# A graph network kernel: node attention with the sources on the partitions, in strips of five destination tiles

## What is computed

```python
def gat_conv(x, src, dst, W, a_src, a_dst, b):
    h = x @ W
    s = h @ a_src
    d = h @ a_dst
    alpha = jax.nn.leaky_relu(s[src] + d[dst], NEG_SLOPE)
    n = h.shape[0]
    m = jax.ops.segment_max(alpha, dst, num_segments=n)
    ex = jnp.exp(alpha - m[dst])
    denom = jax.ops.segment_sum(ex, dst, num_segments=n)
    w = ex / (denom[dst] + 1e-16)
    out = jax.ops.segment_sum(h[src] * w[:, None], dst, num_segments=n)
    return out + b
```

## Time and profile before

| | us |
|---|---|
| median of 3 runs | 5927.24 |
| lowest and highest | 5904.29, 5947.91 |
| span of the profiled execution | 5765.0 |
| `count_edges`, first DVE step to the end of its stores | 792.6 to 1648 |
| node attention, layers 1, 2, 3, first DVE step to the last | 399.9, 401.1, 401.8 |

### The profile page before, as it was taken

One profiled execution on the slowest core, in us unless ns is written; L12 is line 12 of the kernel. 1 busy time (PEld: TensorE's weight loads), 2 busy tenths in 40 slices (PEclk: granted clock), 3 DMA queues, 4 the chain that ended last, 5 costly groups with the idle time before them and its releaser, 6 DMA issues. The chain is left out here.

```text
span 5765.0 us, 88635 instructions
## 1 busy us (share of the span) xinstructions
PE 4607.2 (80%) x24482; PEld 3873.4 (67%) x24483; DVE 2716.3 (47%) x5068; ACT 2120.2 (37%) x3279; POOL 836.5 (15%) x769
## 2 busy tenths in 40 slices
PE   3888868888856499669589989899769959969666
PEld 2677645555545399438578778788659959969555
DVE  5555567777653400321379689689631140020233
ACT  2333215544433200424256566566524420020332
POOL 2778710000005200002100000000022200000000
PEclk8788889999968799789799999999779979989878
DMA  3433311211113342113211111111122134224000
GB/s 97 113 111 106 101 37 71 79 71 75 66 62 100 106 161 109 30 34 116 65 51 56 46 44 55 42 49 55 39 71 97 36 93 162 109 92 159 36 17 24
DMA packets 150165, 438.52 MB, mean 76 GB/s; under 512 B 25592, under 2 KB 89805, under 8 KB 133676
## 3 DMA queue, kind: packets, MB, share of 16 engines
q1 hardware_dynamic: 115212, 341.23, 16.7%
q0 software_dynamic: 34848, 96.08, 5.9%
HBM read 340.98 MB, written 96.25 MB: 76 GB/s over the span
## 5 line engine op out<-in xcount | busy, mean ns | idle before, releaser
L2404 PE MATMUL p_acc<-p_H,p_eT 125*125 125x256 f32 x3750 | 823.5, 378 | 0.0
L2404 PEld LDWEIGHTS p_acc<-p_H,p_eT 125*125 125x125 f32 x3750 | 695.2, 187 | 106.0
L1033 POOL DMA_INDIRECT p_message<-edge_table,p_index x425 | 503.8, 1185 | 131.2 <-issue 120.9
L1951 DVE TENSOR_REDUCE p_mean<-F 128x1 f32<-128x3125 f32 x10 | 34.0, 3403 | 931.7 <-PEq L83 931.7
L1246 PE MATMUL p_acc<-p_message,p_spread 125*125 125x260 f32 x1666 | 425.6, 422 | 28.7 <-issue 28.7
L1298 POOL IOTA p_order_i<- 125x200 int32 x3 | 1.1, 381 | 2882.6 <-SPq L81 2882.6
L1705 ACT ACTIVATE p_hid<-p_up,p_b1s 128x125 f32<-128x125 f32 x764 | 273.0, 366 | 395.6 <-PE p_up L1681 352.5
L1246 PEld LDWEIGHTS p_acc<-p_message,p_spread 125*125 125x125 f32 x1666 | 348.4, 211 | 98.1 <-issue 30.6
L1681 PEld LDWEIGHTS p_up<-p_xT,p_w1s 128*128 128x128 f32 x3056 | 377.8, 199 | 51.3 <-issue 33.1
L1681 PE MATMUL p_up<-p_xT,p_w1s 128*128 128x125 f32 x3056 | 385.5, 283 | 32.9 <-issue 11.8
L835 PE MATMUL p_acc<-p_cell,p_heavy 125*125 (+1 forms) x1440 | 405.4, 392 | 0.0
(11 more groups left out here) (441 smaller groups left out, 8080.0 us busy)
## 6 DMA issues: line engine op xcount, KB each, us to landing
sums_first<-edge_sums SPq DMA_DIRECT2D x48, 1250.0 KB
p_second<-edge_sums SPq DMA_DIRECT2D x48, 1250.0 KB, 6.7
p_count<-edge_counts SPq DMA_DIRECT2D x75, 762.9 KB
edge_sums<-p_sums SPq DMA_DIRECT2D x32, 1250.0 KB, 4.4
edge_counts<-p_total SPq DMA_DIRECT2D x32, 610.4 KB
p_w1s<-in_L_ffn_W SPq DMA_DIRECT2D x16, 1024.0 KB
p_got<-made SPq DMA_DIRECT2D x25, 560.0 KB
p_dst_all<-dst_row SPq DMA_DIRECT2D x25, 531.2 KB
```

The lines of the kernel that those rows point to most:

```text
L1033: pool.indirect_dma_start(message[:, m, k, :], None, table, bass.IndirectOffsetOnAxis(ap=index[:, m, k:k + 1], axis=0)).then_inc(landed[m] ...
L1951: then(dve.tensor_reduce(mean[:, h:h + 1], F[:, h], AX_X, ALU.add))
L2404: last = pe.matmul(acc[:, s, 0:C], eT[:, r % 4, a % 4], H[:, a, 0:C], start=(a == 0), stop=(a == T - 1))
```

## The change

**In `attend_nodes` the matrix is made with the sources on the partitions.** A block of it is 125 sources x 125 destinations, and it goes straight into PE as the stationary side: there are no transposes and no copies behind them. The destinations are taken in strips of 5 tiles (625 columns), the sources in pieces of 5 tiles, so that a layer has 5 strips x 5 pieces = 25 pieces, each of 5 x 5 blocks. The five tiles of a strip accumulate in five PSUM banks. The peak over the sources is still taken with the destinations on the partitions (`mask`, one instruction of 3125 columns per tile, on a bf16 penalty that now comes from DRAM). Two row vectors per strip, peak - d and peak - 0.2 d (`limits`), are turned from the partitions to the columns of all partitions by PE with a diagonal matrix and ones (`spread_limits`), and ACT copies them to `steep` and `flat`. For each block row of 625 columns ACT makes steep - s, not below 0 (`steeps`), DVE takes the minimum with flat - 0.2 s (`join`), ACT makes exp(-x) for a piece (`exponents`), and DVE limits it to 1 and multiplies by the counts (`weigh`). The denominator is a column of ones ahead of H (POOL writes it), so a product has 257 columns. The feature tensor XT serves as two of the four buffers of pieces. H is projected from XT directly, without the copies of L2236.

**In `count_edges`** ACT makes a third copy of each block, `number`, from the same bank as `present`. SP stores `number` as a second table with the sources on the rows (`cells`, 128 x 25 runs of 100 uint16 each per group), and `keeps(j)` waits until the store of group j-1 has landed, since there is one buffer. The turned counts become a penalty, BIG where there is no edge, stored as bf16, and the turning is a bf16 product with the identity.

The diff, with the removed body of `attend_nodes`, the lists of semaphores and small tensors, the unchanged start of the stage and the callers left out:

```diff
--- before.py
+++ after.py
...
-def count_edges(nc, g, counts, weights):
...
@@ -751,9 +751,11 @@
...
-        turned = ph.sb("turned", [P, T, GD])
+        present = ph.sb("present", [P, T, GD], BF16)
+        number = ph.sb("number", [ROWS, T, GD], U16)
+        big = ph.sb("big", [P, 1])
         sums = ph.sb("sums", [ROWS, 2, T, GD])
-        total = ph.sb("total", [GD, N], U16)
+        penalty = ph.sb("penalty", [GD, N], BF16)
...
@@ -780,6 +783,8 @@
...
             dve.memset(sums[:], 0.0).then_inc(cleared, 1)
+            dve.memset(number[:], 0).then_inc(cleared, 1)
+            dve.memset(big[:], BIG).then_inc(cleared, 1)
...
@@ -875,7 +880,7 @@
...
-                        last = pe.transpose(flip[:, f % 4, (h - a) * P:(h - a + 1) * P], turned[:, h], g.ident[0:P, 0:P])
+                        last = pe.matmul(flip[:, f % 4, (h - a) * P:(h - a + 1) * P], present[:, h], ident16[:], start=True, stop=True)
...
@@ -897,14 +902,15 @@
...
-            act.wait_ge(cleared, 1)
+            act.wait_ge(cleared, 3)
             def keeps(j, i, m):
...
+                act.wait_ge(cells_stored, j * 16 + 16)
...
-                    for out, h in ((turned, 0), (sums[0:P, m], 1)):
+                    for out, h in ((present, 0), (number[0:P], 0), (sums[0:P, m], 1)):
                         last = act.activation(out[:, :, s * BLK:s * BLK + BLK].rearrange("p h d -> p d h"),
                                               acc[:, turn_of(nc, b), h, 0:BLK * T].rearrange("p a (d h) -> p (a d) h", h=T), ACT.Copy)
...
@@ -913,7 +919,8 @@
...
-                    act.activation(total[:, a * P:e * P], flip[:, f % 4, 0:(e - a) * P], ACT.Copy).then_inc(flip_kept, 1)
+                    act.activation(penalty[:, a * P:e * P], flip[:, f % 4, 0:(e - a) * P], ACT.Relu, scale=-BIG, bias=big[0:GD, 0:1]).then_inc(flip_kept, 1)
...
@@ -928,6 +935,7 @@
...
+            sp.sem_inc(cells_stored, 16)
...
@@ -935,10 +943,12 @@
...
                     sp.dma_start(weights[bass.ds(j * ROWS, ROWS), :], sums[:, m].rearrange("p h d -> p (h d)")).then_inc(sums_stored[m], 16)
+                    sp.dma_start(cells[:, :, bass.ds(j * GD, GD)], number[:]).then_inc(cells_stored, 16)
...
-                    sp.dma_start(counts[bass.ds(j * GD, GD), :], total[:]).then_inc(stored, 16)
+                    sp.dma_start(absent[bass.ds(j * GD, GD), :], penalty[:]).then_inc(stored, 16)
...
+            sp.wait_ge(cells_stored, 16 * GROUPS + 16)
             sp.wait_ge(stored, 16 * GROUPS + 16)
...
@@ -2134,277 +2144,298 @@
...
-def attend_nodes(nc, g, counts, XT, loads, turn, last, out):
...
+STRIP = 5
+STRIPS = T // STRIP
+SW = STRIP * P
+PIECE = 5
+PIECES_OF = T // PIECE
+MASKS = 8
+SLOTS_OF = 4
+def attend_nodes(nc, g, absent, cells, XT, loads, turn, last, out):
+    PIECES_ALL = STRIPS * PIECES_OF
+    HALVES = ((0, 3 * P), (3 * P, 2 * P))
...
+        H = ph.sb("H", [P, T, C + 3])
...
+        none = ph.sb("none", [128, 2, N], BF16)
...
+        cell = ph.sb("cell", [ROWS, 2, PIECE, SW], U16)
+        room = ph.sb("room", [P, 2, PIECE, SW])
+        gap = (room[:, 0], room[:, 1]) + tuple(XT[0:P, h].rearrange("p (k d) -> p k d", k=PIECE) for h in range(KH))
...
+        flat = ph.sb("flat", [P, 2, SW])
+        diag = ph.sb("diag", [P, 2, STRIP, P])
...
+            def load_none(t):
+                if t >= 2:
+                    sp.wait_ge(masked, t - 1)
+                sp.dma_start(none[:, t % 2], absent[t * P:t * P + 128, :]).then_inc(none_loaded[t % 2], 16)
+            def load_cell(n):
+                k, q = divmod(n, PIECES_OF)
+                if n >= 2:
+                    sp.wait_ge(weighed, (n - 1) * PIECE)
+                sp.dma_start(cell[:, n % 2], cells[:, q * PIECE:(q + 1) * PIECE, k * SW:(k + 1) * SW]).then_inc(cell_loaded[n % 2], 16)
+            load_none(0)
+            load_none(1)
+            load_cell(0)
+            load_cell(1)
+            for t in range(2, MASKS + 2):
+                load_none(t)
+            for n in range(PIECES_ALL - 2):
+                if MASKS + 2 + n < T:
+                    load_none(MASKS + 2 + n)
+                load_cell(n + 2)
...
+            def mask(t):
+                dve.wait_ge(none_loaded[t % 2], (t // 2 + 1) * 16)
+                if t:
+                    dve.wait_ge(masked, t)
+                dve.tensor_tensor_reduce(out=masked_by[:], in0=S[:], in1=none[0:P, t % 2], scale=1.0, scalar=-2.0 * BIG,
+                                         op0=ALU.subtract, op1=ALU.max, accum_out=peak[:, t:t + 1]).then_inc(masked, 1)
+            def limits(k):
+                t = k * STRIP
+                d = H[:, t:t + STRIP, C + 2]
+                dve.wait_ge(masked, t + STRIP)
+                dve.wait_ge(h_kept, t + STRIP)
+                then_small(dve.tensor_tensor(top[:], peak[:, t:t + STRIP], d, ALU.add))
+                then_small(dve.scalar_tensor_tensor(out=top[:], in0=top[:], scalar=0.2, in1=top[:], op0=ALU.mult, op1=ALU.max))
+                then_small(dve.tensor_scalar(any_edge[:], peak[:, t:t + STRIP], -0.5 * BIG, None, ALU.is_ge))
+                then_small(dve.tensor_tensor(top[:], top[:], any_edge[:], ALU.mult))
+                then_small(dve.tensor_tensor(shift[:, 0], top[:], d, ALU.subtract))
+                then_small(dve.scalar_tensor_tensor(out=shift[:, 1], in0=d, scalar=-0.2, in1=top[:], op0=ALU.mult, op1=ALU.add))
+                if k:
+                    dve.wait_ge(limit_spread, 4 * k)
+                for m in range(2):
+                    dve.tensor_tensor(diag[:, m], g.ident[0:P, 0:P].unsqueeze(1).to_broadcast([P, STRIP, P]),
+                                      shift[:, m].unsqueeze(2).to_broadcast([P, STRIP, P]), ALU.mult).then_inc(diag_ready, 1)
+            def join(n, j):
+                t = n % PIECES_OF * PIECE + j
+                o = gap[n % SLOTS_OF][:, j]
+                dve.wait_ge(steep_ready, n * PIECE + j + 1)
+                dve.scalar_tensor_tensor(out=o, in0=flat[:, n // PIECES_OF % 2], scalar=low[:, t:t + 1], in1=o,
+                                         op0=ALU.subtract, op1=ALU.min).then_inc(joined, 1)
+            def weigh(n, lo, hi):
+                o = gap[n % SLOTS_OF][:, lo:hi].rearrange("p k d -> p (k d)")
+                dve.wait_ge(cell_loaded[n % 2], (n // 2 + 1) * 16)
+                dve.wait_ge(raised, n * PIECE + hi)
+                dve.scalar_tensor_tensor(out=o, in0=o, scalar=1.0, in1=cell[0:P, n % 2, lo:hi].rearrange("p k d -> p (k d)"),
+                                         op0=ALU.min, op1=ALU.mult).then_inc(weighed, hi - lo)
...
+            def drain(k, lo, hi):
+                dve.wait_ge(block_used, (k * PIECES_OF + PIECES_OF - 1) * STRIP + hi)
+                then_den(dve.tensor_scalar(den[:, lo:hi], acc[:, lo:hi, 0], 1e-16, None, ALU.add))
+                then_den(dve.reciprocal(den[:, lo:hi], den[:, lo:hi]))
+                for b in range(lo, hi):
+                    dve.scalar_tensor_tensor(out=out[:, k * STRIP + b], in0=acc[:, b, 1:C + 1], scalar=den[:, b:b + 1], in1=b_all[:],
+                                             op0=ALU.mult, op1=ALU.add).then_inc(acc_free, 1)
...
+            for t in range(STRIP):
+                mask(t)
+            limits(0)
+            dve.wait_ge(h_kept, T)
+            then_small(dve.tensor_scalar(minus[:], H[:, :, C + 1], -1.0, None, ALU.mult))
+            then_small(dve.tensor_scalar(low[:], H[:, :, C + 1], 0.2, None, ALU.mult))
...
+            for t in range(STRIP, MASKS):
+                mask(t)
+            for j in range(PIECE):
+                join(0, j)
+            for n in range(PIECES_ALL):
+                k, q = divmod(n, PIECES_OF)
+                if n == 0:
+                    for j in range(PIECE):
+                        weigh(n, j, j + 1)
+                if n + 1 < PIECES_ALL:
+                    if q + 1 == PIECES_OF:
+                        dve.wait_ge(flat_kept, k + 2)
+                    for j in range(PIECE):
+                        join(n + 1, j)
+                if n:
+                    if q == 0:
+                        drain(k - 1, 0, 3)
+                    weigh(n, 0, PIECE)
+                    if q == 0:
+                        drain(k - 1, 3, STRIP)
+                if MASKS + n < T:
+                    mask(MASKS + n)
+                if q == 1 and k + 1 < STRIPS:
+                    limits(k + 1)
+            for b in range(STRIP):
+                drain(STRIPS - 1, b, b + 1)
...
+            def keep_limits(k):
+                act.wait_ge(limit_spread, k * 4 + 4)
+                if k:
+                    act.wait_ge(steep_ready, k * PIECES_OF * PIECE)
+                if k >= 2:
+                    act.wait_ge(joined, (k - 1) * PIECES_OF * PIECE)
+                for m, table in enumerate((steep[:], flat[:, k % 2])):
+                    for h, (lo, n) in enumerate(HALVES):
+                        at = spread[:, 2 * m, 0:n] if h == 0 else spread[:, 1, m * n:(m + 1) * n]
```

(55 more changed lines are left out.)

251 lines of the change are left out of this document (60 added, 191 removed).

## The result

The changed kernel takes 6308.3 us in the median of 4 runs, the kernel before 5937.6 beside it: 1.062 of the time, 95% interval 1.058 to 1.066, **371 us slower**. The prediction was 5835 us, 92 us faster, with a range that ended at 6000.

The account below looks back on a forecast made before the run. PE was taken to bound the attention, and the order of blocks, with no engine full, the counting. Attention -140, counting's start and end +7 and new wait +42 gave -91 from 5927.2: 5835 us, range 5775 to 6000.

Parts of the forecast that it names:

- The attention: Node attention: transposes leave PE, DVE paces the first 17 pieces; 46.5 us gained a layer, 140 us for three.
- The 0.2 us of DVE's waiting per piece: Attention: DVE's waits for its own results, 0.2 us taken off the gain for each of 17 pieces a layer.
- The start and end of the counting: Counting stage: clearing `number`, 2.1 us, and the last penalties queued behind the last counts, about 5 us; 7 us lost.
- the third part of the counting: Counting: ACT's new wait for the previous group's counts store makes a 27.4 us chain against 26.05; 42 us lost.
- the second term: Counting: the loss from waiting on the counts store, 42 us, ranging from nothing to 203 us with the run price.
- t: Counting: DMA engine time of one stored 200-byte run, taken as 28 ns; no profile row had it.
- D: Counting: time from issue of the sums to landing of the counts, 4.4 + 200 t, taken as 10.0 us.
- rival 1: Counting, wait on `cells_stored`: a 200-byte run costs 54 ns like one of 1024 bytes; 5997 us; chance 0.22.
- the chain of the prediction: Counting: copies, store landing and PE's next blocks closing round a group; 17.4 us without D, 27.4 with it.
- The doubled price: Counting: a small store costs a read and a write, twice 54 ns; chain 43 us, about 6330 us; chance 0.04.
- Rival 2: Attention: DVE instructions cost full duration plus 0.2 us waiting, 51 us more in three layers; 5887 us; chance 0.20.
- rival 3: Counting: small stored runs as cheap as the load's, no wait, turns give 19 us back; 5775 us; chance 0.13.

Follow-up runs that it names:

- two_numbers: Changed kernel with two buffers of `number`, so copies no longer wait for the previous group's second-table store: 5873.4 us, +118 us to the kernel before.
- wait_only: one_cast with the changed kernel's wait for the second-table store put back ahead of each group's first copy: 5841.5 us against 5888.0 for the kernel before.
- one_cast: Changed kernel with two f32 copies per block, `number` cast once a group by ACT, only that cast awaiting the store: 5628.0 us against 5755.5 before.
- short_masks: one_cast with the 17 masks per layer between attention pieces cut from 3125 to 125 columns: 5605.8 us against 5631.1 for one_cast beside it.

## Why the prediction was wrong

**The attention: right, by its own steps.** 140 us were forecast and the three stages gave 142. PE's first product comes at 3622.05, 56.0 us into the layer (forecast 55.9); a piece takes PE 11.01 to 11.11 us (11.02), five joins 3.98 (3.9), a strip's vectors 2.27 (2.14); the layer is 353.9 us (353.4 was said; the sum's own terms, 49.4 less 17 x 0.2, give a gain of 46.0 and not 46.5, and so 353.9). That it agrees so closely is in part luck. The 0.2 us of DVE's waiting per piece are not there: DVE runs these pieces with hardly a gap. In their place the first two pieces take PE 13.9 us each, where the granted clock is 0.79 and 0.80 (3622 to 3636 and 3636 to 3653), behind 15 us in which PE did next to nothing. The timeline of PE in layer 1 of after shows the gaps where they were expected, behind DVE:

```profile
3622.05 13.95 PE L2418 MATMUL p_acc<-p_H,p_room 125*125 125x257 f32 x50 [14.70 <-DVE p_room L2291]
3639.30 13.88 PE L2418 MATMUL p_acc<-p_H,p_room 125*125 125x257 f32 x50 [3.30 <-DVE p_room L2291]
3653.02 2.27 PE L2410 MATMUL p_spread<-p_diag,ones 125*125 125x375 f32 x8
3655.13 21.85 PE L2418 MATMUL p_acc<-p_H,XT 125*125 125x257 f32 x100
3676.81 11.01 PE L2418 MATMUL p_acc<-p_H,p_room 125*125 125x257 f32 x50
3688.57 11.11 PE L2418 MATMUL p_acc<-p_H,p_room 125*125 125x257 f32 x50 [0.75 <-DVE p_room L2291]
```

**The start and end of the counting: half of it.** 7 us forecast; 503 less 31 x 15.75 = 488 leaves 15. The first group took 12 of them more than before (967.55 to 1018.70 against 792.56 to 831.74). Only 1.1 us of that clears `number`; the five blocks of slow copies, which the forecast had not priced, stand in the same stretch.

**The step that failed** is the price of the copies, in the third part of the counting: "three copies of 0.85, 0.85 and 1.09 (2.79)". The 0.85 was a copy of f32 into f32, and I carried it over to two copies that write 2-byte elements one by one, 200 bytes apart, without bounding it. They cost 1.9 and 2.2 us from start to start, and the f32 copy behind them 1.2: 5.3 us a block. It was wrong twice over, since I also asked only whether a chain through the new wait is longer than the period, and never added up what ACT has to do in a group. With 2.79 that would have been 18 us of 26 and harmless; with the measured 5.3 it is 30.3, and ACT becomes the bound. Those copies alone cost 7.7 us a group (two_numbers), 239 us. Without its 42 us for the wait the forecast's sum is -133; two_numbers, which has the copies and no wait, is at +118.

**The size of the second term.** t was taken as 28 ns. By the price worked out above it is 25 in the early groups and 49 in the late ones. D was to be 4.4 + 200 t = 10.0; the table lands after 10.3 us in the early groups and after 14.2 in the late ones (14.6 to the next copy in the group shown, 1100.23 to 1114.84). So the forecast was right for half of the groups, and rival 1, whose 54 came from the nearest stored row, a little high for the other half. With the mean of 12.3 the chain of the prediction has 29.7 us and loses 113 where it said 42. The estimate of 12 ns that I had worked out from the Trainium skill ("DMA: Bandwidth & Descriptors", Why small descriptors are slow) is two to four times too low for a store of this kind. The Trainium skill (same page, Specifications) speaks of a read-modify-write below 512 bytes. The doubled price as I put it, twice the 54 for 1024, did not come; but 49 is twice the 24 that the line through the two stores gives for 200 bytes, and twice the price of the early groups, so these runs don't rule out such a step in half of the groups.

**The two are more than their sum.** Per group: the copies alone +7.7 (two_numbers against before), the wait alone +3.2 (wait_only against one_cast), both +15.9 (41.9 against 26.0). While ACT has slack, the wait is partly taken out of it; once the copies fill ACT, every microsecond of D that the penalties don't cover is lost. That the period of the changed kernel is nearly ACT's time end to end fits: 26.5 us of copies, 12.4 from the issue of the sums to the next copy, and 1.9 of waiting for PE ahead of later blocks are 40.8 of 41.8. The 5 us a group that the two have above their sum, 155 us, are in neither term of mine. The 32.1 that I expected of wait_only was added up wrongly: it took D from the issue of the second store and added the cast's 2.3 us, but the cast runs while the sums are stored, and the table lands 12.1 us behind their issue in the mean, 9.9 or 14.3 by the kind of group. So counted, the chain is 25.6 or 30.0 us, and in the early groups it binds nothing; why the late groups take 31 to 34, no run shows.

Rival 1 had the right sign and place, and nearly the right price of a run in half of the groups, but its 5997 us lacks the copies. Rival 2 is refuted by the layer's 353.9 us and by short_masks, rival 3 by t, which is 25 ns and more.

## What to carry to other kernels

When a copy changes its output's type or stride, look for a row with that type and that stride. If there is none, bound it from above by several times the plain copy, or let the scattered write be f32 with one unit-stride cast for the whole tile behind it, as one_cast does. Before following a chain through a new wait, sum each engine's work per loop turn: a wait is cheap only on an engine with slack. Here a store in small runs cost next to nothing as long as nobody's buffer waited for it, so give it either a second buffer or a late producer. And read a price in more than one turn of the loop: one group shown had 49 ns a run, the next 25.

## What the hardware showed that was not expected

- ACT reading 500 f32 of PSUM per partition: 1.07 us into f32 400 bytes apart, 0.60 into bf16 at unit stride, 2.37 to 2.43 into bf16 apart (at 400 and at 200 bytes), into uint16 apart 2.75 behind a slow copy and 2.41 behind a quick one. Into f32 at unit stride it is 0.59. So the stride alone costs 0.5 us, the 2-byte type alone nothing, and both together 1.8.
- The f32 copy behind them is slower as well, 1.40 against 1.12 us.
- A stored run of 200 bytes took 25 ns of a DMA engine in one half of the groups and 49 in the other, which differ in their place in the table; a stored one of 1024 takes 54.
- A DVE step of 0.25 us took 2.27 when it started beside POOL's cast of 2.40.
- The same 425 indirect gathers took 626 to 789 us in different runs, and 707 to 755 on one chip, in code that is the same.
